# A four-stage transformer kernel on one core: the next stage's first work issued before the barrier at four seams, and the experts' second biases moved from VectorE to ScalarE and GpSimd

## The chip, the cores and the metric

The kernel runs on one core of a Trainium2 chip. The metric is the device time of one execution in microseconds. TensorE (PE) multiplies, VectorE (DVE), ScalarE (ACT) and GpSimd (POOL) work elementwise, SyncE (SP) only issues DMAs. Each engine runs its own instructions in order, and engines wait for each other on semaphores.

## The reference

Batch 8, 256 rows of 256 features, two layers in fp32; `ctx` is a context of 64 keys per batch.

```python
x = x + tanh(g0) * cross_attn0(layernorm(x), ctx)   # 16 heads of 128, 4 kv heads
x = x + tanh(g1) * ffn0(layernorm(x))
x = x + tanh(g2) * cross_attn1(layernorm(x), ctx)   # own keys too: rope, rms-norm, causal
x = x + tanh(g3) * ffn1(layernorm(x))               # silu(g) * u, 704 wide
# ffn0(h): causal self-attention, then a mixture of 4 experts, 2 of them taken
h = h + attention(layernorm(h, ln1)) @ wo + bo
comb = two largest of softmax(h2 @ w_gate), softmaxed        # h2 = layernorm(h, ln2)
eout = gelu(h2 @ we1 + be1) @ we2 + be2
ffn0 = h + sum_e comb[:, e] * eout[:, e]
```

## The kernel before

Six phases follow each other, each a function that gives one instruction list per engine: `first_stage` (`c0`, the context's keys and values and the first norms), `cross_attention_0` (`x0`), `self_attention` (`f0`), `experts` (`moe`), `cross_attention_1` (`x1`) and `feed_forward` (`ff`). `phase_end` (L109) is a barrier: each of five engines drains, counts the semaphore `bar` up and waits until all five have done so. So there are four seams that the change touches: `x0` to `f0`, `f0` to `moe`, `moe` to `x1`, `x1` to `ff`. `ff` begins behind the last barrier.

The attention phases have 32 items `i` (4 groups of 4 heads by 8 batches). Per item PE projects (`proj`, `proj_q`, `proj_kv`), multiplies scores, turns the probabilities (`p_tr`), attends and projects out (`out_proj`). An fp32 product is done as three fp32r matmuls on a high and a low part (`three`, L283; also L969 to L971, L2035 to L2037, L2360 to L2362). Weights come by strips: SP fetches one into `RAW`, an engine writes its high part to `Wh`, another the rest to `Wl`; the semaphore `split` counts strips. The norms of the next phase's input are made in the last items (`norm.stats`, `inverse`, `rows`, `turn`, then a high and a low part in `XTh` and `XTl`). The last batch's norm can begin only when its last `out_proj` is added, so it stands alone ahead of the barrier.

In `f0`, ACT copies a projection with its halves swapped (`swapped`, L1097), DVE takes it with the cosine (L1240), and GpSimd needs three operations for each of four takes an item (`rotate`, L1388 to L1394). Its constants are fetched by the phase's first DMAs (L923 to L928), and PE, ACT, DVE and POOL all wait for them.

`moe` has 32 items `c` (8 batches by 4 experts). Per item: PE `up(c)` (12 matmuls, L2035 to L2037), issued three items ahead, ACT Gelu (L2133) and high part (L2137), DVE low part (L2197), PE `down(c)` (12 matmuls), DVE `combine` (L2206). DVE also adds bias times gate to the rows that SP has fetched back from `x_spill` (`bias`, L2222, two instructions an item), and per batch `gated` (L2229) and the norm: statistics at item 0 of the next batch, rows at 1, PE's turn at 2, and DVE's low part at 3 (`norm_low`, L2242), which waits for ACT's `norm_high` (L2122). Ahead of item 0, DVE computes the gates, in a chain of some twenty small instructions with two ACT exponentials in it. PE carries out the context's projections in between (L2057, L2065, L2072). GpSimd makes four tables (L2290), splits weight strips and inverts the variances.

```python
for c in range(3):
    up(c)
for c in range(NU):
    if c + 3 < NU:
        up(c + 3)
    down(c)
```

`x1` opens with a chain of its own through all engines: `proj_kv(0)`, `take_kv` (ACT), `inverse_norm_k` (POOL), `rotate_k` (DVE), `proj_q`, `take_q`, `sum_q` (POOL), `squares` (ACT), `q_tr`, `k_tr`, first scores. Its PE then needs `context_values(0)` of GpSimd (L1872) for the first `attend`. In `ff` an item is one of 6 strips of a batch: PE `up` (L2360), ACT Silu (L2393), DVE product (L2413), POOL high and low part (L2432, L2434), and once a batch DVE result and POOL `add` (L2425).

## Time and profile before

| | |
|---|---|
| time, median of 3 runs (lowest to highest) | 1831.43 us (1830.64 to 1831.76) |
| the profiled execution: its time, its span | 1833.69 us, 1831.9 us |
| busy share PE, DVE, ACT, POOL | 94%, 61%, 72%, 58% |
| mean granted TensorE clock | 0.975 of full |
| instructions in the span | 36545 |

The profiled execution's time is taken around the span; the span runs from its first to its last instruction. A line of the timeline gives the start, the duration and, in square brackets, how long the engine had been idle and which engine and line ended that. "PE busy" is not PE at its peak, as ends of matmuls are modelled.

### The profile page before, as it was taken

What the parts mean: (1) busy time and instruction counts of PE and PEld (TensorE: products, weight loads), DVE (VectorE), ACT (ScalarE), POOL (GpSimd) and SP (SyncE); (2) the same over time, 40 slices, a digit from 0 to 9 for tenths busy, and PEclk for the clock granted to TensorE, in tenths of its full rate; (3) what the DMA queues carried; (4) which work ended last, traced back from release to release, by engine and by line L of the source; (5) the groups of instructions that cost most, each with busy time, mean ns of one, the idle gap of its engine ahead of it and who ended that gap; (6) DMA issues with size and microseconds to landing.
All of it is one profiled execution on the core that took longest, in us unless ns stands there. A gap on an engine that the chain in (4) does not pass through costs nothing.

```text
span 1831.9 us, 36545 instructions
## 1 busy us (share of the span) xinstructions
PE 1717.3 (94%) x11584; PEld 1559.8 (85%) x11584; DVE 1118.2 (61%) x3129; ACT 1327.2 (72%) x4300; POOL 1064.2 (58%) x1208
## 2 busy tenths in 40 slices
PE   5999999799999999999989978999999999998798
PEld 3788888588999999999977867888888888888797
DVE  5577778477766666666867774555555555565222
ACT  4677777588888888888855627888888888888211
POOL 4333337699989889899823115444444444454454
PEclk8999999899999999999989989999999999999899
DMA  4000001100000000000011100000000000000000
GB/s 135 18 16 18 16 30 53 53 19 13 18 19 19 18 19 13 19 13 19 13 59 43 29 18 5 12 9 12 9 12 9 12 9 18 14 21 8 9 19 24
DMA packets 29533, 40.69 MB, mean 22 GB/s; under 512 B 4896, under 2 KB 18464, under 8 KB 29216
## 3 DMA queue, kind: packets, MB, share of 16 engines
q1 hardware_dynamic: 29344, 38.35, 6.9%
q8 instruction: 97, 1.59, 0.4%
q14 instruction: 92, 0.75, 0.1%
HBM read 34.14 MB, written 4.19 MB: 21 GB/s over the span
## 4 chain that ended last, share of the span: by engine, by line
PE 65%; ACT 14%; issue 6%; POOL 5%; DVE 4%; DMA 1%; SPq 0%; POOLq 0%; ACTq 0%; DVEq 0%
PE pS L978 4%; PE pF L285 4%; ACT pA L1642 4%; PE pF L287 4%; PE pF L286 4%; PE pA L287 4%; PE pA L285 4%; PE pA L286 3%; PE pA L969 3%; PE pF L671 3%; PE pA L971 3%; PE pA L970 3%; PE pS L650 3%; PE pO L997 3%; ACT x_P L1668 3%
## 5 line engine op out<-in xcount | busy, mean ns | idle before, releaser
L285 PE MATMUL pA<-Wh,XTh 128*128 128x512 f32 (+1 forms) x512 | 221.8, 433 | 5.2 <-DVEq L117 2.9
L1388 POOL TENSOR_TENSOR f_sw<-f_sw,f_sin 128x512 f32<-128x512 f32 x128 | 181.4, 1417 | 44.2 <-ACT f_sw L1097 44.2
L287 PE MATMUL pA<-Wh,XTl 128*128 128x512 f32 (+1 forms) x512 | 189.0, 369 | 0.0
L286 PE MATMUL pA<-Wl,XTh 128*128 128x512 f32 (+1 forms) x512 | 188.0, 367 | 0.0
L1097 ACT ACTIVATE f_sw<-pA 64x512 f32<-64x512 f32 x256 | 151.7, 593 | 35.4 <-PE pA L971 31.5
L1391 POOL TENSOR_TENSOR f_sw<-f_sw,f_RB 128x512 f32<-128x512 f32 x128 | 169.2, 1322 | 10.0
L969 PE MATMUL pA<-XTh,Wh 128*128 128x256 f32 x512 | 163.4, 319 | 8.1 <-DMA wg<-in_w_gate 7.2
L1668 ACT ACTIVATE x_P<-x_P,x_nm 128x192 f32<-128x192 f32 (+1 forms) x256 | 127.9, 505 | 35.8 <-DVE x_nm L1784 35.8
L280 POOL TENSOR_TENSOR Wl<-RAW,Wh 128x256 fp32r<-128x256 f32 (+3 forms) x64 | 60.7, 949 | 155.3 <-ACT Wh L273 155.3
L970 PE MATMUL pA<-XTl,Wh 128*128 128x256 f32 x512 | 145.2, 284 | 0.0
L971 PE MATMUL pA<-XTh,Wl 128*128 128x256 f32 x512 | 145.2, 284 | 0.0
L1895 POOL TENSOR_TENSOR x_QR<-x_QR,x_t 128x512 f32<-128x512 f32 x64 | 82.3, 1286 | 99.9 <-DVE x_QR L1761 99.9
L1118 ACT ACTIVATE f_P<-f_P,f_nm 128x128 f32<-128x128 f32 (+1 forms) x256 | 114.0, 447 | 22.5 <-DVE f_nm L1257 22.2
L1676 ACT ACTIVATE x_P<-x_P,x_rs 128x192 f32<-128x192 f32 (+1 forms) x256 | 116.2, 507 | 7.2 <-DVE x_rs L1792 7.2
L285 PEld LDWEIGHTS pA<-Wh,XTh 128*128 128x128 f32 x512 | 97.9, 191 | 26.3 <-DVEq L117 3.7
L1784 DVE CUSTOM_DVE_ANT_0 x_P<-pS,x_mask,x_nrq 128x192 f32<-128x192 f32 (+1 forms) x256 | 113.3, 480 | 4.5 <-PE pS L1534 3.7
L286 PEld LDWEIGHTS pA<-Wl,XTh 128*128 128x128 f32 x512 | 98.0, 191 | 18.7
L287 PEld LDWEIGHTS pA<-Wh,XTl 128*128 128x128 f32 x512 | 97.5, 191 | 17.3
L978 PE MATMUL pS<-f_kT,f_qT 128*128 128x128 f32 (+1 forms) x512 | 106.2, 330 | 5.7 <-POOL f_kT L1394 5.7
L1257 DVE CUSTOM_DVE_ANT_0 f_P<-pS,f_mask 128x128 f32<-128x128 f32 (+1 forms) x256 | 80.8, 353 | 48.9 <-PE pS L978 47.9
L969 PEld LDWEIGHTS pA<-XTh,Wh 128*128 128x128 f32 x512 | 98.3, 192 | 11.4 <-issue 7.5
L1126 ACT ACTIVATE f_P<-f_P,f_rs 128x128 f32<-128x128 f32 (+1 forms) x256 | 101.6, 448 | 3.1 <-DVE f_rs L1265 3.0
(286 smaller groups left out, 6093.4 us busy)
## 6 DMA issues: line engine op xcount, KB each, us to landing
RAW<-in_w_f SPq DMA_DIRECT2D x32, 256.0 KB, 2.7
RAW<-in_w_x SPq DMA_DIRECT2D x32, 160.0 KB, 2.2
RAW<-in_w_x SPq DMA_DIRECT2D x32, 128.0 KB, 2.1
RAW<-in_w_ff SPq DMA_DIRECT2D x8, 288.0 KB, 2.7
R<-in_x SPq DMA_DIRECT2D x4, 512.0 KB, 7.2
x_spill<-R SPq DMA_DIRECT2D x8, 256.0 KB, 2.0
RAW<-in_w_moe SPq DMA_DIRECT2D x8, 256.0 KB, 2.6
moe_xs<-x_spill SPq DMA_DIRECT2D x8, 256.0 KB, 3.0
```

The source lines that it names most:

```text
L285: e.matmul(o, ah, bh, start=first, stop=False)
L286: e.matmul(o, ah, bl, start=False, stop=False)
L287: return e.matmul(o, al, bh, start=False, stop=last)
L969: e.matmul(o, Wh[g % 2][:, w], xh, start=(k == 0), stop=False)
L970: e.matmul(o, Wh[g % 2][:, w], xl, start=False, stop=False)
L971: ins = e.matmul(o, Wl[g % 2][:, w], xh, start=False, stop=(k == KD - 1))
L978: ins = e.matmul(pS[:, h % 2, OFF[t]:OFF[t] + WID[t]], qT[:, i % 2, h, t * P:(t + 1) * P], kT[:, i % 2, h, 0:WID[t]], start=True, stop=True)
L1097: ins = e.activation(sw[dst, n, :, :], pA[src, n % 2, :].rearrange("p (a n) -> p a n", a=2), ACT.Copy)
L1388: e.tensor_tensor(y, y, bc(sind[:, :], 1, 2), ALU.mult).then_inc(q["swm"], 1)
L1391: e.tensor_tensor(y, y, RB[:, g % 2, 2 * n:2 * n + 2, :], ALU.add).then_inc(q["swb"], 1)
L1668: ins = e.activation(x, x, ACT.Exp, scale=-1.0, bias=nm[:, h, t:t + 1], accum_out=sm[:, h, t:t + 1])
L1676: ins = e.activation(x, x, ACT.Copy, scale=rs[:, h, t:t + 1])
```

## The change

1. Seam `x0` to `f0`: the `f0` constants have tiles and semaphores of their own that live across phases; SP fetches them at item 20 of `x0`. PE issues `proj(0, 0)` in item 31 ahead of `p_tr(31)`, and `proj(0, 1)` ahead of the last `out_proj`.
2. Seam `f0` to `moe`: PE issues `up(0)` and `up(1)` in the last item of `f0`, behind `scores(31, 3)` and behind `p_tr(31, 2)`.
3. `moe`: `bias` leaves DVE. ACT writes bias times gate to a single tile `moe_gb` (`gated_bias`), GpSimd adds it to the rows (`add_bias`). Rows, turn, high and low part of the norm stand one item later each, the low part two. GpSimd's split of a strip moves behind the third add.
4. Seam `moe` to `x1`: `x1`'s opening for items 0 and most of 1 stands in the last items of `moe` and between its last norm's steps; context tiles share the buffers of the head of `x1` for that.
5. Seam `x1` to `ff`: PE issues `ff`'s first two `up` in item 31 of `x1`. Norms 6 and 7 move into `ff` (statistics and rows in batch 0, turns in batch 1, low parts in batch 2). The Silu table is loaded at the end of `x1`, the scales fetched in it.

```diff
 cross_attention_0
             def sp(e):
                 def body(i, s, nxt):
+                    if i == 20:
+                        self_constants(e)
 ...
                     if not last:
                         scores(i + 1)
+                    else:
+                        next_proj(0)
                     p_tr(i)
 ...
+                def next_proj(n):
+                    e.wait_ge(q["qb"], T * NI)
+                    e.wait_ge(q["split"], NI - 4)
+                    e.wait_ge(n1["lo"], 1)
+                    self_proj_qk(e, 0, n)
                 in_order(e, NI, body, 24)
+                next_proj(1)
                 out_proj(NI - 1, (NI - 1) % 2)
 self_attention, pe
+                def next_up(c):
+                    e.wait_ge(q["taken"], NQ * NI)
+                    e.wait_ge(q["split"], NI - 6)
+                    e.wait_ge(q["nlo"], 1)
+                    experts_up(e, c)
                     scores(i, 3)
                     if one:
                         proj(j, 4)
+                    else:
+                        next_up(0)
                     attend(i, 1)
 ...
                     p_tr(i, 2)
                     if one:
                         scores(j, 0)
+                    else:
+                        next_up(1)
 experts, pe
-                for c in range(3):
-                    up(c)
+                experts_up(e, 2)
 ...
-                    if c % E == 2 and c > E:
+                    if c % E == 3 and c > E:
                         norm_tr(c // E - 1)
+                    if c == NU - 4:
+                        e.wait_ge(q["split"], B)
+                        e.wait_ge(q["nlo"], 2)
+                        head.proj_kv(e, 0)
+                    if c == NU - 3:
+                        head.proj_q(e, 0, 0)
+                    if c == NU - 2:
+                        head.proj_q(e, 0, 1)
+                head.proj_kv(e, 1)
+                head.q_tr(e, 0, 0)
+                head.q_tr(e, 0, 1)
                 norm_tr(B - 1)
+                head.k_tr(e, 0)
 experts, act
+                def gated_bias(c):
+                    i, x = c // E, c % E
+                    e.wait_ge(q["xb"], c)
+                    if c == 0:
+                        e.wait_ge(q["bias"], 16)
+                        e.wait_ge(q["comb"], 1)
+                    for t in range(T):
+                        ins = e.activation(gb[:, t, :], b2[:, x * D:(x + 1) * D], ACT.Copy,
+                                           scale=gcomb[:, T * i + t, x:x + 1])
+                    ins.then_inc(q["gb"], 1)
 ...
+                    gated_bias(c)
 ...
+                    if c == NU - 2:
+                        head.take_kv(e, 0)
 experts, pool
+                def add_bias(c):
+                    i = c // E
+                    if c % E == 0:
+                        e.wait_ge(spl[i % 2], 16 * (i // 2 + 1))
+                    else:
+                        e.wait_ge(q["xb"], c)
+                    e.wait_ge(q["gb"], c + 1)
+                    e.tensor_tensor(xsp[:, i % 2], xsp[:, i % 2], gb[:, :, :], ALU.add).then_inc(q["xb"], 1)
 ...
                 for i in range(B):
-                    split(e, raw_in, q["hi"], q["split"], CW_X1, i, i % 2, 1)
-                    if i:
-                        norm.inverse(e, i - 1)
+                    for x in range(E):
+                        c = E * i + x
+                        add_bias(c)
+                        if 6 <= c < 10:
+                            context_inverse(c - 6)
+                        if i and x == 2:
+                            norm.inverse(e, i - 1)
+                        if x == 2:
+                            split(e, raw_in, q["hi"], q["split"], CW_X1, i, i % 2, 1)
 cross_attention_1, pe
+                    if not one:
+                        next_up(e, 0)
                     attend(i, 0)
 ...
                 out_proj(NI - 1, 0)
-                norm_tr(6)
                 out_proj(NI - 1, 1)
-                norm_tr(7)
 feed_forward, dve
                 def body(i, s, _):
 ...
+                        if i == 0 and m == 1:
+                            scale_result()
+                        if i == 0 and m in (2, 3):
+                            norm.stats(e, 4 + m)
+                        if i == 0 and m in (4, 5):
+                            norm.rows(e, 2 + m)
```

How the instructions stand now is shown at three places. The first is SP's queue at the end of `x0` and the start of `f0`; `f_` tiles and `wg` are the constants, `RAW` the weight strips. Before:

```order
L136 DMA RAW<-in_w_f 128x512
L564 DMA x_spill<-R 128x512 x4
L923 DMA f_cos<-in_cosd 128x256
L924 DMA f_sin<-in_sind 128x256
L925 DMA f_mask<-in_mask_f 128x256
L926 DMA f_bqk<-in_f_bqk 128x64
L927 DMA f_bo<-in_f_bo 128x256
L928 DMA wg<-in_w_gate 128x8
```

And now, from item 20 of `x0` on:

```order
L136 DMA RAW<-in_w_x 128x256 x20
L520 DMA f_cos<-in_cosd 128x256
L521 DMA f_sin<-in_sind 128x256
L522 DMA f_mask<-in_mask_f 128x256
L523 DMA f_bo<-in_f_bo 128x256
L524 DMA f_bqk<-in_f_bqk 128x64
L525 DMA wg<-in_w_gate 128x8
L526 DMA f_bv<-in_f_bv 128x512
L136 DMA RAW<-in_w_x 128x256 x4
```

The seven constants left the place behind the last spills and stand ahead of the strip of item 20.

The second is GpSimd at the start of `moe`, behind the barrier. Before:

```order
L2290 TENSOR_TENSOR x_sin<-x_sin,x_w 128x256
L145 CAST Wh<-RAW 128x320
L147 TENSOR_TENSOR Wl<-RAW,Wh 128x320
L145 CAST Wh<-RAW 128x320
L147 TENSOR_TENSOR Wl<-RAW,Wh 128x320
```

And now:

```order
L2370 TENSOR_TENSOR x_sin<-x_sin,x_KR 128x256
L2359 TENSOR_TENSOR moe_xs<-moe_xs,moe_gb 128x512 x3
L145 CAST Wh<-RAW 128x320
L147 TENSOR_TENSOR Wl<-RAW,Wh 128x320
L2359 TENSOR_TENSOR moe_xs<-moe_xs,moe_gb 128x512 x4
```

The adds stand behind the tables and around each split, four a batch.

The third is VectorE at the end of `moe`, from the low part of item 30 on; `n_xn` are norm rows, `x_KR`, `x_tk`, `x_t` and `x_QR` belong to `x1`. Before:

```order
L2197 TENSOR_TENSOR moe_hl<-pT,moe_hh 128x512
L2206 SCALAR_TENSOR_TENSOR R<-pS,moe_comb,R 128x256 x2
L2222 SCALAR_TENSOR_TENSOR moe_xs<-moe_b,moe_gcomb,moe_xs 128x256 x2
L2197 TENSOR_TENSOR moe_hl<-pT,moe_hh 128x512
L2206 SCALAR_TENSOR_TENSOR R<-pS,moe_comb,R 128x256 x2
```

And now:

```order
L2276 TENSOR_TENSOR moe_hl<-pT,moe_hh 128x512
L2285 SCALAR_TENSOR_TENSOR R<-pS,moe_comb,R 128x256 x2
L1616 SCALAR_TENSOR_TENSOR x_KR<-pA,x_ssk,x_cosk 128x128
L1618 SCALAR_TENSOR_TENSOR x_tk<-pA,x_ssk,x_sink 128x128
L1616 SCALAR_TENSOR_TENSOR x_KR<-pA,x_ssk,x_cosk 128x128
L1618 SCALAR_TENSOR_TENSOR x_tk<-pA,x_ssk,x_sink 128x128
L194 TENSOR_SCALAR n_xn<-R,mv,rstd 128x256 x2
L2276 TENSOR_TENSOR moe_hl<-pT,moe_hh 128x512
L2285 SCALAR_TENSOR_TENSOR R<-pS,moe_comb,R 128x256 x2
```

The bias pair is gone, and `rotate_k(0)` with a norm's rows stands ahead of the low part of the last item, for which PE's last `down` waits.

## Rows read from the trace of the kernel before

**Rows 1.** The page, busy time, share of the span and instructions of each engine.

```profile
PE 1717.3 (94%) x11584; PEld 1559.8 (85%) x11584; DVE 1118.2 (61%) x3129; ACT 1327.2 (72%) x4300; POOL 1064.2 (58%) x1208
```

**Rows 2.** Windows by stage: us, PE, PEld, DVE, ACT, POOL busy, PEclk, DMA share, GB/s.

```profile
335.00:953.00 618.00, 595.14 (x4209) 557.90 (x4209) 407.21 (x1261) 502.19 (x1372) 526.71 (x418) 0.99 0.06 18
...
953.00:1092.00 139.00, 120.74 (x848) 109.39 (x848) 107.40 (x255) 67.30 (x160) 27.27 (x44) 0.93 0.15 46
...
1092.00:1711.00 619.00, 590.77 (x3936) 529.52 (x3936) 335.37 (x1104) 502.11 (x1842) 300.02 (x411) 0.99 0.04 12
```

**Rows 3.** Timeline at the first seam: start, us, engine, line, op; in brackets idle before.

```profile
325.41 0.66 PE L660 MATMUL pS<-ident,x_P 128*128 128x128 f32 x4 [2.50 <-DVE x_P L824]
...
330.85 1.97 PE L671 MATMUL pF<-x_VW,x_PT 128*128 128x256 f32 x8 [0.94 <-DVE R L831]
...
339.98 0.55 PE L969 MATMUL pA<-XTh,Wh 128*128 128x256 f32 x1 [7.17 <-DMA wg<-in_w_gate]
...
334.75 0.33 SPq L923 DMA_DIRECT2D f_cos<-in_cosd  x1
...
339.96 0.91 ACT L1105 ACTIVATE f_RB<-f_sin,f_bqk 128x256 f32<-128x256 f32 x2 [11.42 <-DMA wg<-in_w_gate]
...
342.92 1.20 ACT L1097 ACTIVATE f_sw<-pA 64x512 f32<-64x512 f32 x2 [2.05 <-PE pA L971]
...
344.26 1.27 POOL L1388 TENSOR_TENSOR f_sw<-f_sw,f_sin 128x512 f32<-128x512 f32 x1 [11.94 <-ACT f_sw L1097]
```

**Rows 4.** Timeline at the second seam, TensorE, ScalarE and GpSimd.

```profile
930.67 0.70 PE L997 MATMUL pO<-f_PT,f_V 128*128 128x256 f32 x2 [1.21 <-ACT f_PT L1112]
...
967.07 0.39 PE L285 MATMUL pS<-Wh,moe_hh 128*128 128x256 f32 x1 [2.35 <-DVE moe_hl L2197]
...
957.89 0.22 ACT L2127 ACTIVATE moe_v<-moe_v 128x16 f32<-128x16 f32 x1 [4.25 <-DVE moe_v L2184]
...
964.33 0.73 POOL L2290 TENSOR_TENSOR x_cosk<-x_cos,x_w 128x256 f32<-128x256 f32 x1 [16.86 <-DMA x_mask<-in_mask_x]
```

**Rows 5.** Groups by line in the experts, 953 to 1076 us.

```profile
L285 PE MATMUL pS<-Wh,moe_hh 128*128 128x256 f32 x117 | 34.4, 294 | 10.4 <-DVE moe_hl L2197 10.4
...
L2222 DVE SCALAR_TENSOR_TENSOR moe_xs<-moe_b,moe_gcomb,moe_xs 128x256 f32<-128x256 f32 x58 | 26.2, 492 | 3.5 <-DMA moe_xs<-x_spill 3.5
...
L2242 DVE TENSOR_TENSOR XTl<-pF,XTh 128x512 fp32r<-128x512 f32 x6 | 4.1, 691 | 12.8 <-ACT XTh L2122 12.8
```

**Rows 6.** Timeline, an add of 128x512 on GpSimd in the last stage.

```profile
1737.44 1.30 POOL L2425 TENSOR_TENSOR R<-R,ff_y 128x512 f32<-128x512 f32 x1
```

**Rows 7.** Timeline at the third seam, TensorE and VectorE.

```profile
1069.98 0.28 PE L2035 MATMUL pT<-XTh,Wh 128*128 128x256 f32 x1
...
1071.30 0.28 PE L2037 MATMUL pT<-XTh,Wl 128*128 128x256 f32 x1
...
1075.95 0.39 PE L285 MATMUL pS<-Wh,moe_hh 128*128 128x256 f32 x1 [2.23 <-DVE moe_hl L2197]
...
1092.02 0.58 PE L285 MATMUL pA<-Wh,XTh 128*128 128x256 f32 x1 [1.46 <-DVEq L117]
...
1104.79 0.43 PE L1532 MATMUL pS<-x_kT,x_qT 128*128 128x192 f32 x1 [0.47 <-ACT x_kT L1656]
...
1117.41 0.70 PE L1552 MATMUL pO<-x_PT,x_V 128*128 128x256 f32 x2 [2.88 <-POOL x_VS L1872]
```

**Rows 8.** Timeline at the fourth seam.

```profile
1703.26 0.75 DVE L1803 SCALAR_TENSOR_TENSOR R<-pF,tanhg,R 128x512 f32<-128x512 f32 x1 [2.63 <-PE pF L287]
...
1711.46 0.58 PE L2360 MATMUL pA<-XTh,Wh 128*128 128x256 f32 x1 [2.75 <-POOLq L117]
...
1713.97 0.41 PE L2362 MATMUL pA<-XTh,Wl 128*128 128x256 f32 x1
...
1715.34 1.28 ACT L2393 ACT_TABLE_LOAD   x1 [5.33 <-DMA ff_ds<-in_ff_ds]
...
1717.73 0.39 PE L2360 MATMUL pA<-XTh,Wh 128*128 128x256 f32 x1 [1.48 <-DVE ff_h L2413]
```

More of the change, by code:

```diff
@@ L1415, in cross_attention_1, with cross_head @@
+        Head = namedtuple("Head", "q QR qT kT V KR nrq at_p at_qk place proj_kv proj_q q_tr k_tr take_kv squares q_ev k_ev "
+                          "take_q rotate_k context_keys inverse_norm_k sum_k sum_q inverse_norms_q t2")
+        def cross_head(scope, KT, tables):
             cosT, sinT, cosk, sink = tables
             NU, NT = 3, 3
[L1417 to L1421 removed]
@@ L1474, in table, with proj_kv @@
                 return bc(halves(x[:, t, :]), 1, HG)
+            def proj_kv(e, i):
+                g = i // 8
+                if g:
+                    e.wait_ge(q["split"], 8 * (g - 1) + 5)
+                e.wait_ge(q["tq"], pos(T * (i - 1) + 1))
+                for t in range(T):
+                    for k in range(KD):
+                        cc = slice(WKV + k * 2 * HD, WKV + (k + 1) * 2 * HD)
+                        ins = three(e, pA[:, NU * i % 2, t * 2 * HD:(t + 1) * 2 * HD], x_part(XTh, i, k, t),
+                                    x_part(XTl, i, k, t), Wh[(g + 1) % 2][:, cc], Wl[(g + 1) % 2][:, cc],
+                                    k == 0, k == KD - 1)
+                ins.then_inc(q["proj"], 1)
@@ new lines, in proj_q @@
+            def proj_q(e, i, t):
+                g = i // 8
+                if g:
+                    e.wait_ge(q["split"], 8 * (g - 1) + 4)
+                if t == 0:
+                    e.wait_ge(q["tq"], T * i)
+                else:
+                    e.wait_ge(q["tk"], i + 1)
+                for k in range(KD):
+                    cc = slice(k * GW, (k + 1) * GW)
+                    ins = three(e, pA[:, (NU * i + 1 + t) % 2, :], x_part(XTh, i, k, t), x_part(XTl, i, k, t),
+                                Wh[(g + 1) % 2][:, cc], Wl[(g + 1) % 2][:, cc], k == 0, k == KD - 1)
+                ins.then_inc(q["proj"], 1)
@@ L1718, in act @@
                     if two:
-                        take_kv(k)
+                        take_kv(e, k)
                     o_ev(i, 0)
@@ L1955, in build, with experts @@
             f0.close()
-        def experts(scope, KT, VC, kn, tables, mask):
+            f0_const.close()
+        def experts(scope, head, KT, VC, kn, tables, mask):
             name = "moe"
@@ L2435, in body @@
                                         ALU.subtract).then_inc(q["hl"], 1)
+                        if i == 0 and m in (3, 4):
+                            norm.inverse(e, 3 + m)
                         if m == 4 and not (i == 0):
```

648 lines of the change are left out of this document (324 added, 324 removed).

## The prediction

> **What bounds the kernel now.** I read the page first: PE is busy 94% of the span [rows 1], so the time can only fall where PE stands idle. Then the windows by stage: `f0` and `x1` leave PE 23 and 28 of 618 and 619 us, while the 139 us of `moe` leave it 18, at a granted clock of 0.93 [rows 2]. Then the timeline around the four barriers, where most of these holes are, and the groups of `moe`. Two things are to be seen. Inside `f0` and `x1` the pace is set once all engines have started, so an earlier start moves everything behind it by as much. In `moe`, PE's waits inside the stage all end on DVE's low part, 10.4 us in total, and DVE itself waits 12.8 us for ScalarE's norm copy and spends 26.2 us on biases [rows 5]. My sum is made against the profiled execution (1833.69 us) and carried to the median of 1831.43, 2.3 us lower.
>
> **First seam.** The barrier falls at 334.75, SP's first issue behind it; PE has been idle for 7.17 us when it starts at 339.98, released by the last constant's DMA [rows 3]. GpSimd, which has three operations per take and is the engine that `f0` then runs behind, starts at 344.26, 9.5 us after the barrier. In the changed kernel the constants and two projections are there at the barrier. ScalarE writes two bias tiles (0.91) and two swapped halves (1.20), and GpSimd starts 2.1 us after it. That is 7.4 us. What moves ahead of the barrier is 24 matmuls: twelve of this shape take 1.32 plus the last one's step of 0.12, so 1.4 us, at full clock [rows 7] (the first and the last of one such twelve). The first twelve lie in a hole of 2.50, the second delay the last `out_proj`, whose own hole is 0.94 [rows 3]. Delay between 0 and 1.8; I take 0.8. Seven more DMA issues ahead of the strip of item 20 cost SP about the 5 us that lie between 334.75 and 339.98 once, and that strip is wanted an item of 8 us later: nothing, 3 us without that cover. **Sum: 6.6, between 5.5 and 7.5.**
>
> **Second seam.** `up(0)` and `up(1)` take 1.4 us each in `f0`'s last item. The first slot has a hole of 1.21 [rows 4], the second a smaller one; what follows there alternates between PE and ScalarE, so I count 1.2 us of delay. At the start of `moe` they bring nothing: the first Gelu stands behind the gates, for whose second exponential ScalarE waits 4.25 us and which runs at 957.89 [rows 4], and PE's `up` were done by then. But a new wait stands there. `gated_bias(1)` may write the single tile only when GpSimd has added item 0, and GpSimd begins its four tables at 964.33, when constants land [rows 4]. Four tables at 0.73 to 1.0, one add at 1.30 [rows 6], and ScalarE goes on at about 969.2. Queued behind it are Gelu and copy of item 2, so the third low part comes at 972.3 and PE, which waited 2.35 us up to 967.07 before [rows 4], waits some 5 us. `down(2)` follows 0.8 us later than before, and PE restarts at the 1.2 GHz level, as after other holes: there twelve matmuls stretch from 1711.46 to 1713.97, 0.23 apart instead of 0.12 [rows 7, 8]. I put 1.7 us on that. **Sum: minus 3.7, between minus 5.5 and minus 1.5.**
>
> **Inside the experts.** Of the 10.4 us, 2.35 belong to the start [rows 4] and 2.23 to the tail [rows 7]. What is left is 5.8 us; DVE loses 0.9 us of work an item and the wait for the norm copy becomes one item looser. New is ScalarE's pair at 0.91 [rows 3] (the same form), which may make a context evacuation late, so I take 4.5 of it. Between 2 and 6. Each add (1.30, beside PE) is free as long as the ring of tile and add turns faster than PE's item of 24 matmuls, 2.9 us: 0.91 + 1.30 + 0.2 = 2.4. It is close, and a rival below. The adds also bring GpSimd 42 us of work beside VectorE, in a stage where it has only 27 us in 139 now [rows 2], so no row of the stage shows how the two share the memory. The Trainium skill (SBUF — State Buffer, "SBUF: two separate sides") says that VectorE and GpSimd share one port pair as an exclusive lock, which a VectorE operation with two SBUF inputs or in a two-port mode needs too, so that "the other fully blocks". By it the rows and `gated` of each batch could be held up to an add each, which leaves DVE below PE: the sum by the rule is the same but for the case named under the rivals.
>
> **Third seam.** Let 1069.98, the start of `up(31)`, be the zero [rows 7]. Before, the barrier is 22.0 behind it (1092.02), the first scores 34.8 (1104.79), the first `attend` 47.4 (1117.41). The 12.8 us between barrier and scores are what moves into the tail. Two bounds: all of it is hidden (gain 12.8), or none. Against hiding stand the queues. PE's `proj_kv(0)` behind `down(28)` waits for the eighth strip, which GpSimd now splits only behind the third add of batch 7 and an inverse. ScalarE's `take_kv(0)` stands ahead of Gelu(31). DVE's `rotate_k(0)` waits for GpSimd behind the last add, and the low part of item 31, with PE's last `down`, is queued behind it, as the third place of the order shows. After it, the two sums of q and the inverse norms of q run on GpSimd between the last norm's steps. I count five GpSimd operations of about an add's size (1.30 [rows 6]) on a chain that had none of them: split, last add, two sums, inverse norms, 6.5 us. From the barrier to the first `attend` I leave the 12.6 us as they are, since `context_values(0)` still stands behind the sums of item 1. **Sum: 6.3, between 2 and 10.**
>
> **Fourth seam.** The last residual add starts at 1703.26 [rows 8] and the barrier fell 8.2 us later, behind the norm of batch 7, PE at 1711.46. Without that norm the barrier comes about 1 us after the add's start. Two `up` of 1.4 us stand in the last item, with hardly a hole there, but the two last `out_proj` now run back to back without a turn between them; net delay 0.6. Behind the barrier PE next needs only Silu and a product: 1717.73 stands 1.11 us after the end of the table load (1715.34 + 1.28). So that point moves from 1717.73 to about 1706.0, 11.7 us. Given back: the start at 1.2 GHz for the twelve matmuls and a bit (1.3), the scale that now waits on DVE for its DMA (0.4), and two statistics, two rows, two low parts put between DVE's products, at about 0.69 each [rows 5] 4.1 us, of which the products' gaps take over half, and two turns on PE: 2.0. **Sum: 8.0, between 6 and 10.5.** A stalled product is late for PE at once, since `up` runs only two ahead.
>
> 6.6 - 3.7 + 4.5 + 6.3 + 8.0 = 21.7 us: 1812.0 for the profiled execution, **1809.7** for the median. What can be told from no change is about 0.2%, 3.7 us.
>
> **The rivals.** *A knot at the third seam.* The queues above cost the whole 12.8 us, because DVE, ScalarE, GpSimd and PE each wait once for another. For: four waits in a row with work queued behind each. Against: none of them is long by itself. 6.3 us less: 1816.
>
> *DVE held by the adds.* DVE's 107.4 us in `moe` less 28.9 for 64 biases leave 78.5; if each of 32 adds held it 1.30, it would be busy 120 of 139 us, as long as PE [rows 2]. The gain inside the stage goes and 2 us more: 1816. This is the skill's rule taken at its worst; most DVE operations left there read PSUM.
>
> *The ring.* If nothing of it overlaps with GpSimd's other work (27.27 us, 3.4 a batch [rows 2]), a batch takes 4 x 2.41 + 3.4 = 13.0 us against PE's 4 x 24 x 0.12 = 11.5. Over seven batches that costs 10.5: 1820. For: a single tile. Against: ScalarE's Gelu and copy run beside the add.
>
> *Slower.* The same place ends on the other side if an add takes far more than its row: a batch is 7.84 + 4a, and the 21.7 us are gone from a = 1.69 on. At 2.0 us an add a batch takes 15.8, 30 us are lost, and the time is 1840. Against it stands the 1.30 of the same form.
>
> *Freer than counted.* The third seam hides most (10), the second costs 1.5, the fourth brings 10: 1800.
>
> **How the numbers follow.** Forecast 0.62 (its own range 1803 to 1816), knot 0.10, DVE held 0.10, ring 0.08, slower 0.04, freer 0.06. From 1801 to 1819 lie the forecast and its bounds, both cases at 1816 and a part of the other two, a little over 8 in 10. Faster by over 0.2%: all but the slower case and a remainder, 0.94; within 0.2% 0.02; slower 0.04.
>
> **What would show it.** Seam one: GpSimd's first rotation about 2 us behind the barrier. Seam two: the first Gelu as late behind the barrier as now (some 6.6 us), then a ScalarE wait for GpSimd of 5 to 6 us ahead of the second bias pair. Inside: PE's waits for the low part under 2 us between those ends. Third: first `attend` some 41 us behind the start of `up(31)`. Fourth: barrier to the third `up` about 1.2 us. I am wrong if PE's idle time inside `moe` grows, if ScalarE waits for the add in every item, or if the first rotation still waits for a DMA.

## The result, and the profile after

| | before | changed |
|---|---|---|
| time, median of 4 runs | 1831.47 us | 1817.45 us (1814.19 to 1817.73) |
| profiled execution: time, span | 1833.69, 1831.9 us | 1814.19, 1812.3 us |
| busy share PE, DVE, ACT, POOL | 94, 61, 72, 58% | 94, 61, 75, 61% |

The ratio is 0.992, with a 95% interval of 0.9905 to 0.9936: 14.0 us faster. 1809.7 was forecast. The time lies inside the range of 1801 to 1819, and 1.5 us outside the 1803 to 1816 that the prediction gave to its forecast case. Of the forecast 21.7 us 14.0 came. The two profiled executions differ by 19.5 us, since the one of before is 2.2 us above its median and the one of after the fastest of its four.

The page and the windows of the changed kernel, in the columns of [rows 2] (`f0`, and `moe` up to 1076, some 16 us before its barrier):

```profile
PE 1707.6 (94%) x11584; PEld 1556.1 (86%) x11584; DVE 1102.8 (61%) x3067; ACT 1350.6 (75%) x4363; POOL 1100.9 (61%) x1238
```

```profile
331.50:941.50 610.00, 592.73 (x4208) 557.66 (x4208) 407.98 (x1260) 501.52 (x1372) 526.84 (x418) 0.99 0.06 17
941.50:1076.00 134.50, 115.87 (x820) 105.59 (x821) 82.28 (x176) 93.43 (x228) 67.91 (x78) 0.95 0.15 48
```

PE is idle for 17 us in `f0` instead of 23. In `moe`, DVE works less, and ACT and GpSimd 26 and 41 us more than in [rows 2], though this window lacks the tail. From the gates' second exponential to the start of `up(31)`, the same two landmarks in both, PE is idle for 13.8 us instead of 8.5: the prediction's own sign of being wrong inside `moe`. Where the time went is best read from landmarks, the start of one instruction in both timelines. Each column is the distance to the profiled execution of before (minus: earlier); "again" is the first experiment, the same kernel once more.

| landmark | before, us | changed | again |
|---|---|---|---|
| `x0`, item 5 | 108.38 | -2.0 | -1.0 |
| last residual add of `x0` | 332.85 | -3.2 | -2.3 |
| last rotation of `f0` | 921.07 | -11.4 | -10.7 |
| `moe`, second exponential of the gates | 957.89 | -11.3 | -10.7 |
| `moe`, low part of item 4 | 975.47 | -11.4 | -11.1 |
| `moe`, start of `up(31)` | 1069.98 | -7.1 | -6.8 |
| `x1`, first scores | 1104.79 | -13.0 | -11.6 |
| `x1`, first `attend` | 1117.41 | -12.4 | -10.1 |
| `x1`, residual add of item 0 | 1143.66 | -12.3 | -8.9 |
| `x1`, residual add of item 28 | 1657.90 | -11.3 | -7.9 |
| last residual add of `x1` | 1703.26 | -9.1 | -7.4 |
| `ff`, first residual add | 1737.44 | -19.6 | -17.9 |

No instruction ahead of item 5 of `x0` was moved, so the first line is a difference between executions. So is a part of the start of `x1`, where the repeated run loses 2.7 us between the first scores and item 0's add, and this one 0.6. The windows from the first scores on say why, first of this execution, then of the repeated one (PEclk is the third number from the end):

```profile
1091.00:1105.00 14.00, 9.17 (x40) 7.28 (x40) 6.08 (x20) 8.25 (x38) 6.92 (x12) 0.86 0.08 24
1105.00:1140.00 35.00, 33.99 (x212) 30.45 (x213) 18.55 (x61) 27.20 (x99) 15.18 (x21) 0.95 0.04 11
```

```profile
1091.00:1107.00 16.00, 10.64 (x40) 8.32 (x40) 7.40 (x24) 8.34 (x38) 6.87 (x12) 0.76 0.07 21
1107.00:1142.00 35.00, 33.68 (x203) 29.98 (x204) 17.71 (x58) 25.78 (x92) 14.17 (x21) 0.91 0.04 11
```

With PE waiting 4.1, 1.2 and 2.9 us there, the granted clock is lower than full, and by how much differs from execution to execution (the kernel before has 1.00 and 0.95 in the same two stretches): 0.10 of 16 and 0.04 of 35 us are 3.0 us by this estimate, and the repeated execution took 2.8 more (1816.98). So the 1814.19 is the lucky one of its four, and about 3 us of the 19.5 are not in the median. At the seams the timeline of the changed kernel shows:

```profile
327.69 1.89 PE L725 MATMUL pF<-x_VW,x_PT 128*128 128x256 f32 x8
...
331.53 0.91 ACT L1157 ACTIVATE f_RB<-f_sin,f_bqk 128x256 f32<-128x256 f32 x2 [5.05 <-DVEq L117]
...
333.93 1.26 POOL L1440 TENSOR_TENSOR f_sw<-f_sw,f_sin 128x512 f32<-128x512 f32 x1 [3.38 <-ACT f_sw L1149]
...
946.64 0.22 ACT L2196 ACTIVATE moe_v<-moe_v 128x16 f32<-128x16 f32 x1 [4.25 <-DVE moe_v L2263]
957.00 0.91 ACT L2185 ACTIVATE moe_gb<-moe_b,moe_gcomb 128x256 f32<-128x256 f32 x2 [5.26 <-POOL moe_xs L2359]
...
950.39 0.58 PE L290 MATMUL pS<-Wh,moe_hh 128*128 128x256 f32 x1 [4.32 <-DVE moe_hl L2276]
960.01 0.39 PE L290 MATMUL pS<-Wh,moe_hh 128*128 128x256 f32 x1 [1.62 <-DVE moe_hl L2276]
...
1694.20 0.75 DVE L1909 SCALAR_TENSOR_TENSOR R<-pF,tanhg,R 128x512 f32<-128x512 f32 x1 [3.23 <-PE pF L292]
1696.22 0.36 PE L1472 MATMUL pA<-XTh,Wh 128*128 128x256 f32 x1 [2.06 <-DVE ff_h L2510]
```

GpSimd starts `f0` 2.4 us behind the barrier (ACT's first work, 331.53), where it was 9.5 [rows 3]. The wait of the single tile at the start of `moe` is there at 5.26 us. The third `up` of `ff` stands 2.0 us behind the last residual add instead of 14.5 [rows 8].

Inside the experts there is a wait that the prediction named, and for which it took off 1.3 us without working it out. The groups by line of PE, from 941.5 to 1063 us:

```profile
L290 PE MATMUL pS<-Wh,moe_hh 128*128 128x256 f32 x112 | 32.7, 292 | 6.8 <-DVE moe_hl L2276 6.8
L2112 PE MATMUL pO<-ident,x_VC 128*128 128x128 f32 x16 | 2.9, 315 | 6.4 <-ACT x_KT L2167 6.4
```

and its timeline, with ACT's, DVE's and GpSimd's beside it:

```profile
992.86 1.09 PE L2112 MATMUL pO<-ident,x_VC 128*128 128x128 f32 x4 [3.32 <-ACT x_KT L2167]
999.27 0.63 PE L2112 MATMUL pO<-ident,x_VC 128*128 128x128 f32 x4 [1.55 <-ACT x_KT L2167]
...
991.23 0.91 ACT L2185 ACTIVATE moe_gb<-moe_b,moe_gcomb 128x256 f32<-128x256 f32 x2 [1.65 <-POOL moe_xs L2359]
992.05 0.67 ACT L2167 ACTIVATE x_KT<-pO,x_kn 128x512 f32<-128x512 f32 x1
...
1003.79 1.77 DVE L2293 SCALAR_TENSOR_TENSOR R<-R,tanhg,moe_xs 128x512 f32<-128x512 f32 x1
...
1003.74 1.27 POOL L2359 TENSOR_TENSOR moe_xs<-moe_xs,moe_gb 128x512 f32<-128x512 f32 x1 [3.77 <-ACT moe_gb L2185]
```

`context_t` (L2112) transposes one of four context blocks per item, 8 to 11, into a bank that ACT must first empty (L2167). ACT's bias pair now stands ahead of that copy. The first time the pair itself waits 1.65 us for GpSimd, and PE waits 3.32 us; the second and third time PE waits 1.55 us. The kernel before has one such wait, of 0.79 us.

### The profile page after: what moved, and what is told of

Its sections match the earlier page's. It is cut to its first block, busy times and chain, and to the rows that moved or that the text cites. A ratio compares the mean times of both kernels' runs of the same rounds, so it can differ in the third digit from the quotient of the medians.

```text
span 1812.3 us, 36577 instructions
## 1 busy us (share of the span) xinstructions
PE 1707.6 (94%) x11584; PEld 1556.1 (86%) x11584; DVE 1102.8 (61%) x3067; ACT 1350.6 (75%) x4363; POOL 1100.9 (61%) x1238
## 4 chain that ended last, share of the span: by engine, by line
PE 66%; ACT 15%; issue 6%; POOL 5%; DVE 3%; DMA 1%; SPq 0%; POOLq 0%; ACTq 0%; DVEq 0%
PE pS L1019 4%; PE pF L290 4%; PE pF L292 4%; PE pF L291 4%; ACT pA L1583 4%; PE pA L290 4%; PE pA L292 4%; PE pA L291 4%; PE pA L537 3%; PE pA L538 3%; PE pA L539 3%; PE pS L704 3%; PE pO L1038 3%; PE pF L725 3%; ACT x_P L1805 3%
## 5 line engine op out<-in xcount | busy, mean ns | idle before, releaser
L1813 ACT ACTIVATE x_P<-x_P,x_rs 128x192 f32<-128x192 f32 (+1 forms) x256 | 116.0, 506 | 7.1 <-DVE x_rs L1898 7.1
L1902 DVE TENSOR_TENSOR x_OTl<-pO,x_OTh 128x256 fp32r<-128x256 f32 x128 | 54.3, 424 | 82.5 <-ACT x_OTh L1819 79.1
```

Of the source, the lines that this page charges most:

```text
L1813: ins = e.activation(x, x, ACT.Copy, scale=rs[:, h, t:t + 1])
```

## The experiments

All times are medians; the kernel before stood at 1831.3, 1830.9, 1829.5 and 1831.4 us beside them. The four or five single runs of a kernel spread over 1 to 6 us, so differences under 2 us decide nothing. Beside runs 9 to 11 the kernel before was 1.4 to 1.9 us faster than beside the others, so between groups the ratio is the better measure.

| run | what | us | ratio to before (95%) |
|---|---|---|---|
| 1 | the changed kernel again | 1816.98 | 0.9925 (0.9912 to 0.9937) |
| 2 | evacuation ahead of the bias pair | 1808.11 | 0.9886 (0.9869 to 0.9903) |
| 3 | two bias tiles | 1812.74 | 0.9902 (0.9889 to 0.9916) |
| 4 | biases back on DVE | 1807.21 | 0.9874 (0.9861 to 0.9888) |
| 5 | no projection in `x0` | 1817.02 | 0.9931 (0.9915 to 0.9948) |
| 6 | no `up` in `f0` | 1817.09 | 0.9929 (0.9913 to 0.9944) |
| 7 | opening of `x1` behind the barrier | 1815.06 | 0.9920 (0.9905 to 0.9934) |
| 8 | no `up` in `x1` | 1814.34 | 0.9912 (0.9897 to 0.9927) |
| 9 | 2, 3, 7 and 8 together | 1807.91 | 0.9877 (0.9861 to 0.9894) |
| 10 | 4, 7 and 8 together | 1807.05 | 0.9872 (0.9855 to 0.9889) |
| 11 | 2, 3 and 8, two knots out of the opening | 1804.20 | 0.9860 (0.9840 to 0.9880) |
| 12 | 11, and `context_values(0)` first | 1800.76 | 0.9832 (0.9818 to 0.9845) |

**Run 1, no edit.**

> The changed kernel once more, unchanged, as the baseline of the other runs and to see which part of the 19.5 us between the two profiled executions comes back. The median was 1817.45, the profiled execution 1814.19. If the 2 us that the first items of x0 gained ahead of any moved instruction are a difference between executions, they are gone here and GpSimd's first rotation of f0 stands about 8.5 us ahead of the kernel before instead of 10.3. If they belong to the change (a longer program loads otherwise), they are here again.

1816.98 us. `x0` stands 1.0 ahead at item 5 in this execution, 2.1 ahead in run 2 and 0.2 behind in run 4, all with the same code up to there: up to 2 us at that place belong to the execution. The first rotation is 9.4 ahead.

**Run 2, the evacuation first.**

```diff
-                    gated_bias(c)
+                    if c not in range(12, 16):
+                        gated_bias(c)
 ...
                     if 12 <= c < 16:
                         context_t_ev(c - 12)
+                        gated_bias(c)
```

> ScalarE empties the bank of a context transpose ahead of the bias pair of the same item, in items 12 to 15; nothing else. Theory 1 (the pair stands in front of the evacuation for which PE waits): PE's three waits for it, 3.32, 1.55 and 1.55 us, fall to about 1.0, 0.65 and 0.65, and the time falls by 4 us, to about 1813. Theory 2 (DVE is held by GpSimd's adds): no change, within 1 us. Theory 3 (the ring of the single tile sets the pace): no change, since the ring turns as before.

8.9 us faster, twice what theory 1 gave. The three waits are 0.76 each, the first of them:

```profile
990.03 0.63 PE L2112 MATMUL pO<-ident,x_VC 128*128 128x128 f32 x4 [0.76 <-ACT x_KT L2167]
```

That is 3.9 us of waiting less than in run 1. From the gates' second exponential to the start of `up(31)` the stage takes 110.5 us instead of 116.0, 5.5 less, since a hole of 3.3 us has a price behind it: the windows of the changed kernel ahead of it and behind it,

```profile
980.00:989.40 9.40, 9.40 (x81) 9.33 (x79) 8.55 (x18) 8.05 (x25) 6.67 (x9) 1.00 0.17 48
992.80:996.00 3.20, 3.14 (x15) 3.17 (x16) 0.28 (x1) 0.00 (x0) 0.82 (x1) 0.52 0.00 0
```

show a granted clock of 1.00 and then 0.52, the 1.2 GHz level, for 3.2 us: about half of them, 1.6 us, are lost. Together with the 3.9 us of waiting that gives the 5.5. The other 3 us of the 8.9 come from the start of `x1`: from `up(31)` to the add of item 0 run 1 takes 71.6 us, this run 67.5. Theory 1 holds for the stage, and its forecast of 4 us left out the clock; 2 and 3 can't give this, since the edit changes neither DVE's work nor the ring.

**Run 3, a second tile.**

```diff
-                    e.wait_ge(q["xb"], c)
+                    e.wait_ge(q["xb"], pos(c - 1))
 ...
-    e.tensor_tensor(xsp[:, i % 2], xsp[:, i % 2], gb[:, :, :], ALU.add).then_inc(q["xb"], 1)
+    e.tensor_tensor(xsp[:, i % 2], xsp[:, i % 2], gb[c % 2], ALU.add).then_inc(q["xb"], 1)
 ...
                 e.wait_ge(q["cte"], 4)
+                e.wait_ge(q["xb"], NU)
```

> Two tiles for bias times gate, so that ScalarE may run one item ahead of GpSimd's add (the second tile lies in a tile of x1 that is free until the end of the stage). Theory 1: ScalarE's wait of 5.26 us at the start and of 1.65 us in item 12 go; PE's first wait for the evacuation falls from 3.32 to about 1.7, the two of 1.55 stay: 1.5 to 2 us faster. Theory 3: most of the 5 us that the stage loses come back: 4 to 5 us faster. Theory 2: nothing, within 1 us.

4.2 us faster, the size that theory 3 gave and twice that of theory 1. The places decide between them. 4.5 us are gained between the exponential and `up(31)`. 1.4 of them are there at item 4 (15.8 against 17.2 us), the price of the 5.26 us wait at the start. 3.2 are there when PE restarts behind its first wait for the evacuation, and all 4.5 when it restarts behind the second: PE waits 1.55 us three times, as theory 1 said, and with the first wait its stretch at the 1.2 GHz level is gone too. From there to `up(31)`, some 15 items, nothing is gained, where a ring that set the pace would have given something in every item. So the single tile cost something, but only at the start and in item 12; in the changed kernel ACT waited 10.2 us in all for GpSimd's 32 adds.

**Run 4, the biases back on DVE.** `gated_bias` and `add_bias` are taken out, `bias(c)` stands behind `combine` as in the kernel before.

> The biases back on DVE as in the kernel before, with everything else of the change kept (the norm one item later, the split behind, all four seams). It prices the second half of the title. Theory 1: PE's waits for the evacuation fall from 6.4 to under 1 us, and its waits for the low part return to at most 4 us: 1 to 4 us faster than the changed kernel. Theory 2: DVE's gated (0.75 or 1.78 us) and rows (0.73 or 1.7) all go back to 0.75, and the time falls by 5 us. My own prediction said 4.5 us slower than with the biases moved, from which the start gives back 2.5.

9.8 us faster than the changed kernel. PE's waits for the evacuation are 2.3 us, those for the low part, up to `up(31)`, 4.1, of which nearly all is the wait for the gates at the start. The groups by line of DVE in the stage, of this run:

```profile
L2306 DVE SCALAR_TENSOR_TENSOR R<-R,tanhg,moe_xs 128x512 f32<-128x512 f32 x8 | 6.2, 779 | 0.1
L194 DVE TENSOR_SCALAR n_xn<-R,mv,rstd 128x256 f32<-128x256 f32 x14 | 5.5, 438 | 0.0
```

and of the changed kernel:

```profile
L194 DVE TENSOR_SCALAR n_xn<-R,mv,rstd 128x256 f32<-128x256 f32 x12 | 8.6, 755 | 0.0
L2293 DVE SCALAR_TENSOR_TENSOR R<-R,tanhg,moe_xs 128x512 f32<-128x512 f32 x7 | 8.6, 1222 | 0.5
```

Beside the adds DVE's `gated` takes 1222 ns on the mean instead of 779, and its rows 755 instead of 438: 7 times 0.44 and 12 times 0.32, 6.9 us. The one of 1.77 us above begins 0.05 behind the start of an add of 1.27 and ends 0.55 behind that add's end, where alone it takes 0.75. The trace fits the exclusive lock of the Trainium skill (SBUF — State Buffer, "SBUF: two separate sides"), which the prediction cited, within 0.2 us. It did not bound the kernel: run 2 keeps all adds and is 0.9 us from run 4 in the medians. But its stage is 3.5 us longer (110.5 against 107.0 us), and what DVE's longer operations cost in it no run took apart.

From the exponential to `up(31)` this run takes 107.0 us, the kernel before 112.1. **With the biases where they were, the stage is 5.1 us shorter.** The two `up` issued ahead bring 1.2 of it (run 6), and the opening of `x1` nothing (run 10 has none of it and takes 106.9). What is left of the change there is the norm one item later, with GpSimd's split behind the third add. The trace fits: up to `up(31)` DVE's waits for ScalarE's norm copy fall from 11.0 to 2.6 us, and PE's for the low parts, the start left out, from 4.7 to 0.2. The norm's order was not undone alone. Moving the biases then cost 9 us of the 116. Run 9, with the evacuation first and two tiles, takes 109.1, so 6.9 of the 9 are these two queues; the cause of the last 2 is open.

**Run 5, no projection in x0.** The two `next_proj` are out; `f0` begins with all its projections.

> The changed kernel without the two projections that PE issues in item 31 of x0; the constants still come early. Theory A (the projections are half of the seam's gain, and in the hole of item 31 they also keep PE's clock up): the two last out_proj of x0 stretch to some 3.3 us again instead of 1.9 and the last residual add of x0 stands 0 to 1 us later, the barrier is followed by twelve matmuls at 1.2 GHz (2.5 us) before ScalarE's first swapped half; GpSimd's first rotation stands 3.5 us later than in the changed kernel, and the time is 3 to 4 us above its 1817.0. Theory B (the constants alone bring the gain, the projections cost in x0 what they save): no change, within 1 us.

1817.02 us: no change. In the trace theory A is right at the seam. The last two groups of `out_proj` take 2.73 and 1.97 us, the last residual add of `x0` stands 1.3 us later and the first rotation 2.6 us later than in run 1. But at the last rotation 0.36 us of the 2.6 are left. PE, ACT and DVE lose the head start in two places. The first is behind a wait of PE for GpSimd's `f_kT`, of 2.50 us in run 1 and 2.51 in run 5. These are the windows of the same `proj` behind it, of run 1 and of run 5:

```profile
409.80:413.30 3.50, 3.50 (x17) 3.41 (x16) 1.82 (x6) 0.99 (x4) 3.34 (x4) 0.51 0.02 5
```

```profile
412.30:414.30 2.00, 2.00 (x18) 1.95 (x17) 1.85 (x6) 0.99 (x4) 1.84 (x3) 1.00 0.03 8
```

Run 1 is granted the 1.2 GHz level there and run 5 full speed, and run 5 makes up 1.6 us. The second place is the low part of a norm. The timelines of DVE and GpSimd, of run 1:

```profile
427.86 1.61 DVE L272 TENSOR_TENSOR XTl<-f_xa,XTh 128x512 fp32r<-128x512 f32 x1
429.40 1.77 DVE L1351 TENSOR_TENSOR R<-R,f_bo 128x512 f32<-128x512 f32 x1
...
444.21 1.29 POOL L1440 TENSOR_TENSOR f_sw<-f_sw,f_sin 128x512 f32<-128x512 f32 x1 [2.08 <-ACT f_sw L1149]
```

and of run 5:

```profile
428.80 0.68 DVE L272 TENSOR_TENSOR XTl<-f_xa,XTh 128x512 fp32r<-128x512 f32 x1
429.40 1.76 DVE L1348 TENSOR_TENSOR R<-R,f_bo 128x512 f32<-128x512 f32 x1
```

In run 1 the low part is held for 0.9 us beside GpSimd's work, in run 5 it slips through, and from 429.40 on both executions stand at the same time. GpSimd, which stays some 2.6 ahead until 441, then waits 2.08 for ScalarE at 444.21. That the lock sets who is held fits the rows. Whether other executions lose the head start at the same places is not shown; the medians of the two runs are the same.

**Run 6, no up in f0.** Both `next_up` are out, `moe` starts with `for c in range(3)`.

> The changed kernel without up(0) and up(1) in the last item of f0; all three stand at the start of moe again. My prediction: 1.2 us faster, since they cost that in f0 and bring nothing behind the barrier, where the first Gelu waits for the gates. The trace of the changed kernel shows no loss in f0 (11.4 us ahead at the last rotation, 11.3 behind the barrier), which expects no change, within 1 us. A rival, that the two up keep the clock up into the barrier and shorten the chain of the gates: 1 us slower or more.

1817.09 us: no change. But it is a balance of two terms and not two times nothing. From the last rotation of `f0` to the gates' second exponential this run takes 36.2 us, run 1 36.9: the two `up` cost up to 0.7. From there to the low part of item 4 it takes 18.4 us, run 1 17.2: they bring 1.1. Both differences are of one execution each, and the 0.7 is the weaker one, since the kernel before has no such `up` either and takes 36.8. The rival, that they shorten the chain of the gates, is not borne out: that chain stands in the first stretch.

**Run 7, the opening of x1 behind the barrier.** All calls of `head.` leave `moe` and stand at the head of `x1`, on each engine in the order of the kernel before.

> The opening of x1 stands behind the barrier again, on all engines in the order of the kernel before; the last norm, the biases and everything else as in the changed kernel. Sum of the prediction: 6.3 us slower than the changed kernel. The trace: from the start of up(31) to the first attend the changed kernel takes 5.3 us less than the one before, in which the waits of the tail (2.1 for the last weight strip, 2.1 for the low part of item 31) are already counted: 5 to 6 us slower, 1822 to 1823. The rival (a knot of waits that gives the gain back): within 1 us of the changed kernel.

1815.06 us; it was to be 5 to 6 us slower and is no slower. So the 5.3 us that the changed kernel gains between `up(31)` and the first `attend` (42.2 against 47.4 us) don't come from the opening: this run takes 42.0. The timeline of PE in run 7:

```profile
1063.74 0.36 PE L554 MATMUL pT<-XTh,Wh 128*128 128x256 f32 x1
...
1072.76 0.28 PE L290 MATMUL pS<-Wh,moe_hh 128*128 128x256 f32 x1
1078.25 0.63 PE L202 MATMUL pF<-ident,n_xn 128*128 128x128 f32 x4 [4.54 <-DVE n_xn L194]
1093.14 0.59 PE L1695 MATMUL pS<-x_kT,x_qT 128*128 128x192 f32 x2 [0.47 <-ACT x_kT L1597]
1105.74 0.45 PE L1715 MATMUL pO<-x_PT,x_V 128*128 128x256 f32 x1 [2.86 <-POOL x_VS L1988]
```

and in the changed kernel:

```profile
1062.88 0.36 PE L554 MATMUL pT<-XTh,Wh 128*128 128x256 f32 x1
...
1068.09 0.39 PE L290 MATMUL pA<-Wh,XTh 128*128 128x256 f32 x1 [2.09 <-POOL Wl L147]
1074.70 0.39 PE L290 MATMUL pS<-Wh,moe_hh 128*128 128x256 f32 x1 [2.09 <-DVE moe_hl L2276]
1082.62 0.39 PE L290 MATMUL pA<-Wh,XTh 128*128 128x256 f32 x1 [1.81 <-ACT pA L1583]
1086.21 0.63 PE L1558 MATMUL pT<-ident,x_QR 128*128 128x128 f32 x4 [1.46 <-POOL x_QR L1641]
1091.84 1.01 PE L1695 MATMUL pS<-x_kT,x_qT 128*128 128x192 f32 x2 [4.10 <-POOLq L117]
1105.04 1.13 PE L1715 MATMUL pO<-x_PT,x_V 128*128 128x256 f32 x2 [2.87 <-POOL x_VS L1970]
```

Run 7 is through with its last `down` 9 us behind `up(31)`, the kernel before 14.1, since the low parts of the last items no longer come late. The changed kernel needs 17.0, with the opening's matmuls and three waits in it, and is at the scores 29.0 us behind `up(31)`, run 7 at 29.4. The opening is hidden, and as much is lost in front of it.

The wait of 2.09 us for `moe_hl` is not where the prediction and the expectation put it. The low part at 1073.97 is that of item 30, which stands ahead of `rotate_k(0)`. ScalarE and DVE in the changed kernel:

```profile
1069.83 0.28 ACT L1575 ACTIVATE x_sk<-pA 128x128 f32<-128x128 f32 x1 [5.79 <-PE pA L292]
1072.75 0.58 ACT L2191 ACTIVATE XTh<-pF 128x512 fp32r<-128x512 f32 x1
...
1073.37 0.69 DVE L2306 TENSOR_TENSOR XTl<-pF,XTh 128x512 fp32r<-128x512 f32 x1 [6.45 <-ACT XTh L2191]
1073.97 0.68 DVE L2276 TENSOR_TENSOR moe_hl<-pT,moe_hh 128x512 fp32r<-128x512 f32 x1
```

PE waits 2.09 us for the last weight strip, so `proj_kv(0)` is late. ScalarE's `take_kv(0)` waits for it for 5.79 us, and Gelu(31), a bias pair and the norm copy of `norm_high` stand behind it. DVE's `norm_low` waits 6.45 us for that copy, and the low part of item 30 is queued behind `norm_low`. That is the knot, and `rotate_k` has no part in it.

**Run 8, no up in x1.**

> The changed kernel without the two up that PE issues in item 31 of x1; the norms of the last two batches stay in ff. The trace shows x1 11.3 us ahead until item 30 and 9.1 at its last residual add: the two up cost 2.3 us there, 0.6 in my prediction. Without them those 2.3 come back, and behind the barrier the two take 2.5 us at 1.2 GHz plus Silu and product ahead of the third up. Theory A (they only move work): no change, within 1 us. Theory B (they are what makes the start of ff short): 2 to 3 us slower. Theory C (the 2.3 us in x1 are more than they bring): 1 to 2 us faster.

1814.34 us, 2.6 below run 1; the intervals overlap. By the landmarks 1.9 of it are there at the add of item 28, where the code is the same. From there to the last residual add the changed kernel loses 2.2 us against the one before and run 1 loses 0.5 (7.9 to 7.4 ahead), while run 8 gains 0.6 (9.8 to 10.4). From the last add to the first of `ff` it takes 25.2 us instead of 23.6. So the two `up` cost 1.2 to 2.8 us in `x1` and bring 1.6 in `ff`: theory A within what can be told, and theory C is not ruled out.

**Runs 9 and 10, the single results together.**

> Evacuation first and two tiles (as in the second and third run), the opening of x1 behind the barrier again, and no up in item 31 of x1; biases on ScalarE and GpSimd. If the single results add: 1817.0 less 8.9, less 1.9, less 2.7 is 1803.5, and the second tile may give 1 more (its 4.2 us overlap with the 8.9, since both remove the wait of item 12). If the pieces only shift waits around, it stays at 1806 or above.

> Biases on DVE, the opening of x1 behind the barrier again, no up in item 31 of x1: of the change only the constants, the four up and projections in f0 and x0, the norm one item later and the norms of ff are left. Adding single results: 1807.2 less 1.9, less 2.7 is 1802.6. With the opening gone from the tail, DVE's biases stand in nobody's way but PE's waits for the low part return there (up to 3.4 us in the kernel before): 1803 to 1805.

1807.9 and 1807.1 us: 4 us above the sum in both, and no better than runs 2 and 4 alone. The parts of the sum were not what they seemed: some 3 of the 8.9 us and most of the 1.9 and 2.7 are, by the landmarks, run 1's slow start of `x1`, which each single result had counted again.

The pair shows something else. From the exponential to `up(31)` run 9, with the biases on ScalarE and GpSimd, takes 109.1 us and run 10, with them on DVE, 106.9. From `up(31)` to the first `attend` it is 42.7 against 44.9: in run 10 PE waits 0.98, 1.70 and 1.12 us for the last low parts. So the moved biases do shorten the tail, by the same 2.2 us that they still cost before it, and the whole is even.

**Run 11, the opening with two knots out.**

```diff
                 for c in range(NU):   # dve
-                    if c == NU - 2:
+                    if c == NU - 1:
                         head.rotate_k(e, 0)
 ...
+                        if c == NU - E:   # pool
+                            split(e, raw_in, q["hi"], q["split"], CW_X1, i, i % 2, 1)
                         add_bias(c)
```

> Evacuation first, two tiles, no up in item 31 of x1, and the opening of x1 kept in the tail of moe, with two of its knots taken out: GpSimd splits the last weight strip ahead of batch 7's adds (PE waited 2.1 us for it), and DVE's rotate_k(0) stands behind the low part of item 31 (which waited behind it, 2.1 us for PE). If waits of the tail are what ate the opening's gain: 4 us below the same kernel without the opening, under 1800. If they only move on to the next wait (PE for take_kv 1.8, for GpSimd's sum 1.5, 4 us at the barrier): within 1 us of it, 1802 to 1804.

1804.20 us, 3.7 below run 9. PE's wait for the weight strip is gone. The wait of 2.1 us for a low part is not, since it is for the one of item 30 (run 7): ScalarE's `take_kv(0)` waits for PE, its norm copy starts at 1063.81, and DVE's `norm_low` and low part follow at 1064.43 and 1065.04. And the wait for `rotate_k`, which now stands one low part later, grew from 0.6 to 2.1:

```profile
1065.77 0.39 PE L290 MATMUL pS<-Wh,moe_hh 128*128 128x256 f32 x1 [2.07 <-DVE moe_hl L2276]
1069.61 0.50 PE L290 MATMUL pA<-Wh,XTh 128*128 128x512 f32 x1 [2.14 <-DVE x_tk L1618]
1083.65 1.01 PE L1695 MATMUL pS<-x_kT,x_qT 128*128 128x192 f32 x2 [3.81 <-POOLq L117]
```

From `up(31)` to the scores it is now 27.4 us, 2.7 less than in run 9. With the strip's knot out the opening pays; the edit of `rotate_k` took out no wait that was there.

**Run 12, context_values(0) first.** In `x1`, GpSimd's `context_values(0)` moves from behind the sums and inverse norms of item 1 to its first place.

> The run before (evacuation first, two tiles, opening in the tail with its two knots out, no up in item 31 of x1), and in x1 GpSimd makes context_values(0) (1.2 us) ahead of the sums and inverse norms of item 1, in a gap of 2.9 us in which it waits for DVE anyway. PE's wait for it ahead of the first attend (2.87 us, in the kernel before and in every variant) goes. If x1 keeps its pace from its first item on: 2.9 us at the first attend and 2 to 3 us in the time, 1801 to 1802. If x1 gives a head start back, as f0 did with the 2.6 us of its projections: 1804, within 1 us.

1800.76 us, the fastest of all, 30.7 us (0.9832) below the kernel before and 16 below the changed one. PE and GpSimd in its timeline:

```profile
1095.67 0.60 PE L1715 MATMUL pO<-x_PT,x_V 128*128 128x256 f32 x2
...
1088.16 1.19 POOL L1966 TENSOR_SCALAR x_VS<-x_VC,x_half 128x128 f32<-128x128 f32 x2
1090.87 1.29 POOL L1641 TENSOR_TENSOR x_QR<-x_QR,x_t 128x512 f32<-128x512 f32 x1 [1.52 <-DVE x_QR L1607]
```

The 2.87 us in front of the first `attend` are gone, the 1.19 us lie in a gap of GpSimd, and where run 12 was 1.2 us behind run 11 at the first scores it is 1.2 ahead at the add of item 0. So 2.4 of the 2.87 us were kept, and they stay through `x1`. Another 1.6 come behind the add of item 28, where the code is the same. By the ratios, 0.9860 and 0.9832, the step is 5 us, in the medians 3.4.

## Why the prediction was right, and where it was not

**First seam (6.6).** Behind the barrier 7.1 us came where 7.4 were counted, by the steps given. The delay of 0.8 in item 31 was wrong in sign: the projections fill PE's hole, `out_proj` stays at full clock (1.89 us instead of 3.29), and 1.2 to 1.3 us are gained. So the seam shows 8.3 at the first rotation. The constants alone bring what is kept of it: run 5 has no projections and the same time. The premise that an earlier start of `f0` "moves everything behind it by as much" failed for their 2.6 us, 1.6 of them by the clock and 0.9 by a held low part.

**Second seam (-3.7).** The wait came as written, 5.26 us ahead of the second bias pair, and the first Gelu as late as before. Its price was too high: run 3 finds 1.4 us for the wait, where 2.5 were put. And it doesn't show: from the exponential to item 4 the changed kernel takes 17.4 us, the one before 17.6. What fills it are mostly the two `up` issued ahead, which were to bring nothing there and bring 1.1, for 0 to 0.7 in `f0` where 1.2 were put (run 6). Run 4, without the wait, is 1.4 us shorter there than the kernel before.

**Inside the experts (+4.5).** This is the step that failed. From the exponential to `up(31)` the stage grew by 4.2 us. The prediction wrote that the pair at 0.91 "may make a context evacuation late" and took 1.3 of 5.8 us off for it, without working out what stands behind it. That was the bound: 6.4 us of waits instead of 0.8, with the clock behind them (run 2, 5.5 us). The gain was there, but mostly not from the biases: the stage is 5.1 us shorter with them left on DVE, 1.2 of it by the `up` issued ahead and the rest, by the trace, by the norm's order (run 4).

**Third seam (6.3).** 5.3 was measured in the profiled execution, so the size looks right, but that is luck, since its reason fell. Without the opening the same 5.4 are there (run 7), from low parts that no longer come late; with the biases on DVE only 2.5 of them are (run 10), so about half is the moved biases' own. The opening itself brought nothing: the rival of the knot, which I gave 0.10, is what happened in the changed kernel. The strip, `take_kv(0)` and GpSimd's sums were in it, as named; the low part that waits is that of item 30, behind ScalarE's queue, and not that of item 31 behind `rotate_k`. The 12.6 us that the prediction left as they are run from the first scores to the first `attend`, not from the barrier.

**Fourth seam (8.0).** 8.3, from 11.3 ahead at item 28 of `x1` to 19.6 at the first add of `ff`, by other terms. From the last residual add to the third `up` of `ff` the seam gained 12.5, where 12.3 were counted (11.7 with the delay of 0.6 taken off). What is given back behind it, clock, scale and norms together, was 1.9 instead of 3.7, and the two `up` cost 0.6 to 2.2 in `x1` instead of 0.6 (the repeated and the first execution). The norms moved into `ff` were not undone alone.

DVE held by the adds was real (6.9 us of its time) and at most a small part of the path. The ring did not set the pace: ACT and GpSimd kept up after the start. That the time fell inside the range is in part luck: the experts' 8.7 us below their term were partly met by 1.7 and 3.8 us above theirs at the first two seams. About 3 us of the median are the clock at the start of `x1`, which had no term. The case "freer" adds up to 1802, not to the 1800 written there.

What stays open: the constants and the norm's order were not undone alone, 2 of the 9 us that the moved biases cost inside the experts have no cause, and why `x0`'s first items differ by up to 2 us between executions was not looked into.

## What to carry to other kernels

Before work is put on an engine that idles on the mean, look at what stands behind it in that engine's queue and who waits for it: here one copy behind a pair of 0.91 us cost 5.5 us, more than the 4.5 that the whole move was to bring, and its place in the queue, not its amount, was the price. When an edit bundles several moves, undo each alone, since a landmark between two of them credits the neighbour (the opening of `x1` had the gain of the low parts), and before a wait is taken out, count which item it belongs to. The work issued ahead of the barriers here paid little: the projections, the two `up` in `f0` and the two in `x1` changed the time by nothing that could be told when each was taken out. A wait such as PE's 2.87 us for `context_values(0)`, in sight in the profile all along, was worth 2.4 us in the trace and 3.4 in the medians.

## What the runs showed of the hardware

- VectorE operations with SBUF inputs can take about 1 us longer beside a GpSimd operation of 1.27 to 1.30: 1.77 against 0.75 us for one 128x512, 1.70 against 0.73 for a pair of 128x256.
- A head start of 2.6 us in a stage of 580 was gone after 110: 1.6 us behind a PE wait of 2.50, where the granted clock was 0.51 for 3.5 us, and 0.9 at one such held operation. In the other execution the clock behind the same wait was 1.00.
- A wait of PE can cost more than its length, and not the same in every execution: behind 3.32 us of it the granted clock was 0.52 for 3.2 us, behind 1.55 and 2.09 us 1.00, and at the start of `x1` one code had a mean of 0.86 or 0.76 for 14 to 16 us.
